# Sorted picks, sums rank by rank, and products of three widths in an attention and mixture-of-experts kernel

## The reference, cut to what matters

```python
x = x + wkv(time_decay, time_first, layernorm(x), ctx)   # x: 8 x 128 tokens x 256 channels
h = rmsnorm(layernorm(x)) * norm_w                        # 1024 tokens
scores = softmax(h @ gate_w.T)                            # 32 experts
w4, id4 = top_k(scores, 4);  w4 = w4 / sum(w4)            # 4096 picks
buf[expert, pos] = h[token]        # at most 256 rows for an expert
act = silu(buf @ w13_gate) * (buf @ w13_up)               # 256 -> 128, per expert
eo  = act @ w2                                            # 128 -> 256, per expert
out = x' + sum over a token's 4 picks of w4 * eo + shared expert(h)
```

## Time and profile before

| | us |
|---|---|
| median of 3 executions (lowest, highest) | 234.11 (232.91, 234.96) |
| span of the profiled execution, first to last instruction | 228.0 |
| what the median lies above that span | 6.1 |
| expert rows loaded, first transposes | 82.08 |
| first scatter of an expert's result | 90.64 |
| last one ends | 201.97 |

### The profile page before, as it was taken

The page is one execution under the profiler, slowest core; times in us unless marked ns, Lnnn a source line. Parts: engine busy times, 40 slices in busy tenths (PEclk is TensorE's granted clock), DMA queues, the critical chain, the costliest instruction groups (busy, mean ns, idle before and its releaser), DMA issues.

```text
span 228.0 us, 3659 instructions
## 1 busy us (share of the span) xinstructions
PE 139.5 (61%) x819; PEld 119.8 (53%) x819; DVE 120.4 (53%) x385; ACT 84.8 (37%) x254; POOL 115.6 (51%) x140
## 2 busy tenths in 40 slices
PE   1124887787774879969895948858499479200000
PEld 0112765676663559959794837837398377100000
DVE  2878999997433344555253531536237055303990
ACT  3165678566563024434214231335225032002410
POOL 6201156888877500754563736555464646632740
PEclk9999996555555799988999788999979958755555
DMA  5999999998222264775775657465665731129930
GB/s 173 334 340 340 338 339 364 365 373 301 96 99 95 95 198 134 235 204 153 218 198 176 192 161 220 136 189 158 185 172 171 232 115 52 43 69 359 385 122 23
DMA packets 40270, 46.46 MB, mean 204 GB/s; under 512 B 4585, under 2 KB 37045, under 8 KB 40252
## 3 DMA queue, kind: packets, MB, share of 16 engines
q1 hardware_dynamic: 35200, 37.30, 53.2%
q0 software_dynamic: 4608, 8.54, 10.5%
q10 hardware_dynamic: 444, 0.40, 0.5%
HBM read 27.95 MB, written 22.45 MB: 221 GB/s over the span
## 4 chain that ended last, share of the span: by engine, by line
PE 36%; issue 20%; SPq 19%; another core or an unknown queue 7%; DVE 7%; DMA 5%; ACT 2%; POOL 0%; POOLq 0%; ACTq 0%; DVEq 0%
PE bank L882 18%; PE bank L899 11%; SPq L204 10%; PE bank L874 8%; SPq L227 5%; DVE part L769 4%; DMA G<-rows_out 3%; DVE act_t L730 1%; ACT xT L476 1%; DMA xg<-rows_in 1%; ACT sg L481 1%; DVE res L769 1%; SPq L210 1%; DMA rows_out<-yo,pick_idx 1%
## 5 line engine op out<-in xcount | busy, mean ns | idle before, releaser
L333 POOL DMA_INDIRECT rows_out<-yo,pick_idx x64 | 62.6, 978 | 55.7 <-issue 47.8
L882 PE MATMUL bank<-xT,w13b 128*128 128x128 f32 x368 | 51.6, 294 | 8.5 <-issue 5.6
L882 PEld LDWEIGHTS bank<-xT,w13b 128*128 128x128 f32 x368 | 48.1, 208 | 11.0 <-issue 11.0
L476 ACT ACTIVATE xT<-bank,cols 128x256 f32<-128x256 f32 x64 | 26.8, 473 | 43.0 <-PE bank L874 37.0
L899 PE MATMUL bank<-w_all,act_t 128*128 128x256 f32 x92 | 29.7, 434 | 16.0 <-DVE act_t L730 14.9
L730 DVE TENSOR_TENSOR act_t<-sg,bank 128x256 f32<-128x256 f32 x32 | 13.5, 421 | 49.3 <-ACT sg L481 36.5
L318 POOL DMA_INDIRECT rows_in<-n_row,slot_all x32 | 32.5, 1015 | 10.0 <-issue 10.0
L481 ACT ACTIVATE sg<-bank 128x256 f32<-128x256 f32 x32 | 12.3, 386 | 44.6 <-PE bank L882 25.1
L899 PEld LDWEIGHTS bank<-w_all,act_t 128*128 128x128 f32 x92 | 16.5, 209 | 18.8 <-issue 17.9
L737 DVE COPY yo<-bank 128x512 f32<-128x512 f32 x32 | 22.0, 687 | 6.6 <-remote 3.3
L874 PE MATMUL bank<-ident,xg 128*128 128x128 f32 x128 | 22.0, 301 | 1.3 <-DMA xg<-rows_in 1.2
(11 more groups left out here) (109 smaller groups left out, 194.3 us busy)
## 6 DMA issues: line engine op xcount, KB each, us to landing
rows_in<-zeros SPq DMA_DIRECT2D x32, 264.0 KB, 6.4
xg<-rows_in SPq DMA_DIRECT2D x32, 264.0 KB
w13b<-in_L_ffn_w_dram SPq DMA_DIRECT2D x32, 256.0 KB
w_all<-in_L_ffn_w_dram SPq DMA_DIRECT2D x4, 1024.0 KB
G<-rows_out SPq DMA_DIRECT2D x7, 512.0 KB, 7.1
rows_out<-yo,pick_idx POOLq DMA_INDIRECT x64
x_all<-in_x_dram SPq DMA_DIRECT2D x1, 768.0 KB, 5.2
v_all<-in_ctx_dram SPq DMA_DIRECT2D x1, 768.0 KB, 7.6
```

The source lines that it names most:

```text
L333: pool.indirect_dma_start(rows_out, bass.IndirectOffsetOnAxis(ap=pick_idx[:, q, a:a + 1], axis=0), yo[:, q, a, :], None, bounds_check=PICK ...
L476: act.activation(xT[:, j, h, :], FX[j][:, h, :], ACT.Copy, scale=nw[:, h:h + 1]).then_inc(s["f_x"], 1)
L882: last = nc.tensor.matmul(FG[q % 2][:, a, cols], w13b[q][:, h, a, :], xT[:, q % 2, h, cols], start=(h == 0), stop=(h == HC - 1))
```

## The change

- **Picks sorted by expert.** A token's four experts are ordered from the highest number down (one DVE maximum over 8 values, straight into the row's tags); the pick numbers are laid out by rank, so that `rows_out` holds rank by rank. The softmax weights are worked out once for all blocks, and put into the same order by seven DVE operations during expert 2.
- **Experts from 31 down to 0.** Rank 0 of every token is then settled after 29 experts, rank 1 after 30, and so on. SP loads a rank of `G` (1 MB, the last in four parts) when its experts' scatters have landed and all `yo` are made.
- **All weights stay in SBUF** in 12 loads of 1 MB, 8 of them issued in stage 1 (before: 1 MB of `w13` and 4 MB of `w2` there, and 256 KB per expert in the loop); `yo` and `G` lie over used weights, pick numbers have 32 buffers, `xg` 6. No loops are left: all programs are unrolled.
- **PE.** The second two transposes run only where the expert has over 128 rows; gate and up run at 128, 192 or 256 columns, chosen by two branches. The flags are loaded once.
- **Sums.** DVE sums blocks 0 to 3, PE blocks 4 to 7 in PSUM with diagonal matrices of the weights (made by ACT in the loop); ACT copies and stores these.

```diff
-POOL_SUMS = (1, 3, 6)
+MORE = 3 * P // 2
+SETTLED = E - K + 1
+XB = 6
+        def expert(i):
+            return E - 1 - i
+
+        def settles(i):
+            return max(i - (SETTLED - 1), 0)
...
+            for r in range(K):
+                sp.wait_ge(row_out[r], 32 * SETTLED if r == 0 else 32)
+                if r == 0:
+                    sp.wait_ge(s["f_yo"], E)
...
+                if r < K - 1:
+                    sp.dma_start(G[r], ranked[K - 1 - r].rearrange("(b p) c -> p b c", p=P)).then_inc(gathered[r], 16)
+                else:
+                    for c in range(SUMS_DVE):
+                        sp.dma_start(home[:, :, c, :], rows[:, :, c, :]).then_inc(last_gathered[c], 16)
...
-            run([(-2, exp_k), (3, negative_max), (2, shifts), (2, normed), (3, pick_weights), (0, first_reciprocal),
-                 (2, normed_T), (3, shared_to_sbuf), (3, tag_rows), (2, base)])
+            run([(-2, exp_k), (2, shifts), (2, normed), (0, first_reciprocal),
+                 (2, normed_T), (3, shared_to_sbuf), (2, base)])
+            act.wait_ge(s["expo_done"], 1)
+            act.activation(ew[:, :, :], expo[:, :, :], ACT.Exp).then_inc(s["ew_ready"], 1)
             act.wait_ge(s["gu_done"], B)
             act.activation(sg_all[:, :, :], gu_all[:, 0], ACT.Silu).then_inc(s["sh_s"], 1)
...
+            def rows_to_channels(e, j, second):
+                pe.wait_ge(xg_in[e % XB], 16 * (e // XB + 1))
                 with pe.If(second != 0):
+                    transpose_half(e, j, 1)
+                transpose_half(e, j, 0).then_inc(s["f_xt"], 1)
...
+                with pe.If(third != 0):
+                    gate_up_slots(e, j, CAP)
+                with pe.Else():
+                    with pe.If(second != 0):
+                        gate_up_slots(e, j, MORE)
+                    with pe.Else():
+                        gate_up_slots(e, j, P)
...
+            for e in range(AHEAD):
+                picks_of_slots(e)
+            for e in range(E):
                 gated(e, e % 2)
                 if e:
-                    rows_out_to_sbuf(e - 1, e - 1, 0)
+                    rows_out_to_sbuf(e - 1)
+                if e + AHEAD < E:
+                    picks_of_slots(e + AHEAD)
+                if e == 2:
+                    weights_in_order()
...
+            for q in range(B - SUMS_DVE):
+                nc.tensor.matmul(FT[q], ident[:, :], base_all[:, SUMS_DVE + q, :], start=True, stop=False)
...
+                    last = nc.tensor.matmul(FT[q], diag[:, q, r, :], G[r][:, SUMS_DVE + q, :], start=False,
+                                            stop=(r == K - 1))
```

More of the change, by code:

```diff
@@ L213, in load_rows @@
[L213 to L225, removed]
@@ L226, in _, with load_rows @@
-            for g in range(W2L):
-                sp.dma_start(w2_all[:, g * n:(g + 1) * n, :], w2[g * n:(g + 1) * n].rearrange("e p c -> p e c"))\
-                    .then_inc(w2_in[g], 16)
+            for g in range(EARLY):
+                load_w13(g)
+                if g % 2 == 0:
+                    load_w2(g // 2)
+            def load_rows(i):
+                first = expert(i) * ROWS_E
+                sp.dma_start(xg[i % XB][:, :, :], rows_in[first:first + CAP, :].rearrange("(a p) c -> p a c", p=P))\
+                    .then_inc(xg_in[i % XB], 16)
@@ L229, in _, with store_last @@
+            def store_last(m):
+                lo, hi = (E // 2, E) if m == 0 else (0, E // 2)
+                sp.dma_start(last_rows[lo:hi].rearrange("(o e) c -> o e c", o=1),
+                             w13_all[P - 1:P, lo:hi, 1].rearrange("p e a f -> p e (a f)")).then_inc(last_stored[m], 16)
             for b in range(B):
                 sp.wait_ge(scattered[b], 16 * K)
[L231 to L243, removed]
@@ L259, in _ @@
[L259 to L269, removed]
@@ L339, in _ @@
             flag = pool.value_load(overflow[0:1, 0:1], min_val=0, max_val=1)
-            with pool.Fori(0, E // WB) as i:
-                for q in range(WB):
-                    scatter_out(WB * i + q, q)
+            for i in range(E):
+                scatter_out(i, expert(i))
             with pool.If(flag != 0):
-                for q in range(WB):
-                    pool.wait_ge(last_stored[q], 16 * E // WB)
+                for m in range(2):
+                    pool.wait_ge(last_stored[m], 16)
                 for m in range(B * K):
@@ L677, in _ @@
             dve.wait_ge(s["tot_ready"], 1)
-            dve.tensor_scalar(big[:, :], TOT, CAP / 2 + 0.5, None, ALU.is_gt).then_inc(s["big_done"], 1)
+            dve.wait_ge(s["bit_set"], 5)
+            for m, rows in enumerate((P, MORE)):
+                dve.scalar_tensor_tensor(out=halves[:, m, :], in0=TOT, scalar=rows + 0.5, in1=bit[:, :], op0=ALU.is_gt,
+                                         op1=ALU.mult).then_inc(s["halves_done"], 1)
+            dve.wait_ge(s["halves_done"], 2)
+            with nc.allow_low_precision("sums of different powers of two below 2^16"):
+                dve.tensor_reduce(big[:, :, :], halves[:, :, :].rearrange("p m (g n) -> p m g n", n=BITS), AX.X, ALU.add)\
+                    .then_inc(s["big_done"], 1)
             for c in range(B // 2):
@@ L720, in picks_of_slots @@
+            def picks_of_slots(i):
+                rows, e = xg[i % XB], expert(i)
+                dve.wait_ge(xg_in[i % XB], 16 * (i // XB + 1))
+                dve.scalar_tensor_tensor(out=own[:, e], in0=rows[:, :, TAG:TAG + K], scalar=iota_e[:, e:e + 1],
+                                         in1=rows[:, :, PICK:PICK + K], op0=ALU.is_equal, op1=ALU.mult)\
                     .then_inc(s["own_done"], 1)
-                dve.wait_ge(s["own_done"], e + 1)
-                dve.tensor_reduce(owned[:, q], own[:, q], AX.X, ALU.add).then_inc(s["owned_done"], 1)
@@ new lines, in _ @@
+            for r in range(K):
+                if r < K - 1:
+                    pe.wait_ge(gathered[r], 16)
+                for q in range(B - SUMS_DVE):
+                    if r == K - 1:
+                        pe.wait_ge(last_gathered[q], 16)
+                    last = nc.tensor.matmul(FT[q], diag[:, q, r, :], G[r][:, SUMS_DVE + q, :], start=False,
+                                            stop=(r == K - 1))
+                    if r == K - 1:
+                        last.then_inc(s["tile_summed"], 1)
```

395 lines of the change are left out of this document (196 added, 199 removed).

## The result

The changed kernel took **218.08 us** (median of 4 executions, 216.21 to 221.18), the kernel before 233.51 (232.23 to 234.96): a ratio of **0.935, 95% interval 0.928 to 0.942**. The forecast was 217. The profiled execution took 218.0 us, with a span of 216.3.

The account below looks back on a forecast made before the run. Stage 2 was taken as POOL's 81.8 us of scatters plus 29.8 starving on held PE signals. First scatter 91.0, stage 2 105.4, tail 14.3 give 210.7 span; 6.1 outside makes 217 us, own range 210 to 225.

Parts of the forecast that it names:

- Stage 1: Ahead of the first result scatter: POOL's row scatters set the pace and stay; first result scatter at 91.0 us (89 to 93).
- The exponential ahead of the silu: End of stage 1: exponential and silu table load move behind DVE's last slot numbers, about 2.8 us later; first transposes at 84.3.
- Stage 2: First to last result scatter: 111.3 us less 4.9 (PE) and 3.0 (landed scatters), plus 2.0 for branches, gives 105.4.
- Half of PE's 9.9 us: Stage 2: fewer transposes and narrower products save PE 9.9 us; half, 4.9, counts, as signals are held the rest.
- The wait for landed scatters: Stage 2: DVE's `own` waited for old scatters to land; that wait goes, saving 3.0 us.
- Stage 3: Behind the last scatter: rank-by-rank loads, 2 us to begin, 11.7 us transfer, then product, copy, hand-offs and store: 14.3 us.
- The closing wait: Kernel end: the 3.5 us wait after the last store goes, since POOL finishes long before; bounds 0 and 3.5.
- Outside the span: Median time of the kernel before lies 6.1 us above its profiled span of 228.0; carried over unchanged.
- The hold: Stage 2: PE's signals seem held while POOL scatters back to back, let go about 1.2 us after; 29.8 us of starving.
- POOL becomes the bound: Rival, stage 2: late signals come from register waits or old buffers; POOL runs without pauses, 190 us; chance 0.16.
- half-way case: Rival, stage 2: half of POOL's 29.8 us of pauses gone, about 203 us; chance 0.10.
- PE at the lower clock: Rival, stage 2: PE throttled throughout, 130 us of loop work at half clock, 240 us, slower; chance 0.08.

Follow-up runs that it names:

- e1: The changed kernel with one small POOL multiplication (128x8 numbers by 1) behind its last result scatter: 217.48 us, ratio 0.921 to the kernel before.
- e2: The kernel before with one more partition all-reduce as POOL's last instruction: 250.99 us, ratio 1.056.
- e5: The changed kernel as it is, run again on chip A: 226.17 us, ratio 0.954 to the kernel before.
- e8: e1 with all four transposes and 256-column products for every expert, most row-count branches dropped: 215.02 us, ratio 0.912 to the kernel before.
- e10: e7 with the four ranks of results read back only when the last has landed, on chip B: 184.40 us, ratio 0.895 to the kernel before.
- e3: e1 with a POOL memset of 128x896 numbers behind the two result scatters of every expert: 219.41 us, ratio 0.926 to the kernel before.
- e7: e4 with a POOL memset of 128x448 numbers behind each expert's scatters, on chip A: 190.70 us, ratio 0.810 to the kernel before.
- e9: The kernel before with a POOL memset of 128x896 numbers behind every expert's two scatters, on chip B: 224.47 us, ratio 1.090.
- e4: e1 with an expert's second scatter only above 128 rows (always for the last three), 46 to 48 scatters instead of 64: 198.14 us, no ratio interval.
- e6: e3 with the memset between experts cut from 128x896 to 128x8 numbers: 216.00 us, ratio 0.919 to the kernel before.
- e12: e7 with all four transposes and 256 columns for every expert, without those branches, on chip B: 197.32 us, ratio 0.957.

## Why the prediction was right, point by point

The number was right by terms that cancel, and so by luck: +8.2 (start), -5.2 (stage 2), +2.6 (tail), -4.3 (outside the span) make the +1.3 from 216.8 to 218.1.

- **Stage 1, forecast 91.0 us for the first result scatter, measured 99.2.** The step that failed is the first sentence, that row scatters pace it and nothing else changes. POOL's last sums in the kernel before (L372) had a second effect that I did not see: they brought back the code that the all-reduce had displaced, and the next execution began with it loaded. The change takes POOL's sums away, and its next execution waits 8.98 us ahead of the first IOTA (e1, e2, e5). The question could have been asked: the kernel before has an all-reduce on POOL and sums behind it, and the change drops the sums. By the Trainium skill (GPSIMD Engine Reference, Instruction dispatch) the first call of a newly loaded POOL kernel costs about 6 us that no instruction in the profile shows; the traces agree in kind, with 8.98 and 11.27 us at the start, and in size for e2's all-reduce, with 5.75. That the code stays loaded from one execution to the next is what e1 and e2 add.
- **The exponential ahead of the silu, forecast +2.2 us.** From the end of the last row scatter to the first transposes: 4.5 us before, 5.8 after (85.80 to 91.58), so +1.3.
- **Stage 2, forecast 105.4, measured 100.2.** That POOL starves in pauses behind its runs was right: 11 pauses, 18.8 us beyond the usual gaps (17 and 29.9 before). *Half of PE's 9.9 us* was wrong: even 26.0 us more, with branches dropped, cost nothing (e8). For the *branches* at 2.0 us I have no separate number. The wait for landed scatters went, as said, but 3.0 us for it was too little: 11.1 us were gained in stage 2 (9.7 between e2 and e1 on chip A, 112.6 and 103.0), and by e8 PE's smaller products were hardly a part of it. Nor did deeper buffers let PE run further ahead: when an expert's first scatter starts, at most 2 results lie ready before and 1 after, and PE's gate and up products are at most 3 experts ahead in both. What gave the gain stays open; the waits of `own` (7.4 us to 0), the flag loads, the weight loads and the hardware loops went together, and no run changes one of them alone.
- **Stage 3, forecast 14.3 us behind the last scatter, measured 16.9.** The last rank is asked for 5.1 us after the last scatter's end, not 1.3: that scatter lands late. The 2 us to begin had no row behind them: the first rank was asked for at 195.34 and its first sum begins at 202.07, 6.7 us later, of which 2.9 are transfer at 358 GB/s. The closing wait went as said. Reading rank by rank is worth about the 5.1 us counted on, from 3.8 us ahead of the last scatter's end instead of 1.3 behind it (4.8 to 6.2, e10).
- **Outside the span, 6.1 us carried over, measured 1.7 to 1.8.** Of the kernel before I had one span and the median of other executions. In every run since, time and span of one execution are 1.7 to 1.8 us apart; the rest of the 6.1 was that the profiled execution was the quicker one.
- **The hold itself.** e3 shows that on chip A PE's pace is lost to POOL's unbroken scatters, by 33 us against e1. But the loop of e7 and e10 is the same program, with 5 late starts on one chip and none on the other, and so are their unbroken row scatters. So the scatters alone do not make signals late; something of the chip, or of its state then, has to be added, and that stays open. One difference more is in the traces: of the 96 updates of PE's semaphores e7's lacks 18 and e3's 41, e10's none. Every execution was recorded with span and clock, so whether the recording has a part in the hold can't be told. Instruction fetches, another candidate, are in e10 as in e7 (11 on each of two queues of their pages).
- **The rivals.** *POOL becomes the bound* is what chip B seems to do with the kernel before. The 203 us of the half-way case do not follow from its condition: 91.0 + 81.8 + 14.9, a tail of 11.5 to 14.3 and 6.1 give 205 to 208. *PE at the lower clock* did not come (0.89 over the loop), though e8 shows the other side of it: work that fills pauses can be free because it keeps the clock. What the changed kernel does on chip B was not run; from these parts (e9's loop without its memsets, 8.2 us at the start, a tail 9 us shorter) an estimate is 206 us, no gain there.

## What to carry to other kernels

Look at what every removed operation did for its neighbours, and for the next execution: here POOL's last sums reloaded its code for the next execution, and one operation of 0.27 us beside the tail gives about 8 us back. When one engine's pauses come from another's unbroken runs, ask what that engine costs by itself: breaks alone gained no time, even where they freed PE (e3 219.4 us, against 217.5 in e1), 18 scatters fewer gave 19 us (e4), and with a break of 0.5 us behind each expert some 26 (e7), where 26 us of PE's work were worth nothing beside 64 scatters (e8). And time both kernels on more than one chip before a gain is put down to the code: the same kernel before took 207 us on one and 237 on another.

## What the runs showed of the hardware that I had not expected

- POOL keeps its loaded code from one execution to the next: 0.28 us ahead of the first IOTA where an ordinary operation came last, 8.95 to 11.27 where the all-reduce was the last that was no scatter (the changed kernel, e5, e2).
- POOL's closing DRAIN takes 6.4 to 8.7 us where an ordinary operation or the all-reduce comes late, and can be the end of the kernel (before and e2, and by 0.4 us e1).
- While POOL issues scatters without a break, other engines start on PE's results up to 5.2 us late (before), 3.9 in the changed kernel, 4.3 in e6, where memsets of 0.13 us stand between them; with 0.87 us behind every two scatters no start is over 1 us late (e3). On chip B none is in the loops, which all have breaks (e9 to e12), and in stage 1, which in e10 has none, no engine waits for "remote".
- Added matmuls can keep the granted clock up: it was 0.87 in e1's loop and 1.00 in e8's with 26.0 us more work, PE was busy only 9.0 us more, and the loop was no longer (100.2 against 103.0).
